# Seven block products in place of eight for the first layer of experts 1 to 7

## The chip, the cores and the metric

The kernel runs on one core of a Trainium2 chip. The metric is the device time of one execution in microseconds (us); a run gives one time, and a kernel's time is the median of its runs. The engines are PE (TensorE), DVE (VectorE), ACT (ScalarE), POOL (GpSimd) and SP (SyncE, which only issues transfers here). Each takes its instructions from a queue in the order in which the program wrote them; semaphores order the engines among each other.

## What is computed

Attention over 8 batches of 512 tokens with 256 features comes first, then a soft mixture of 8 experts with 128 slots each. The change is in the experts' part, which in the reference reads:

```python
slots = jnp.einsum('bnd,bnes->besd', xn, dispatch)
h = jnp.einsum('besd,edh->besh', slots, w1) + b1[None, :, None, :]
h = jax.nn.gelu(h, approximate=False)
eo = jnp.einsum('besh,ehd->besd', h, w2) + b2[None, :, None, :]
out = jnp.einsum('bmd,bnm->bnd', eo.reshape(b, e * s, DIM), combine)
```

For one expert, h is a product of 8 x 128 slot rows with 256 features and a w1 of 256 x 1024; eo multiplies it with a w2 of 1024 x 256.

## The kernel before

Matmuls take float32r. For accuracy each value is split in a rounded high part and the rest, and a product is made of three passes, high x high, high x low, low x high (`PASSES`). ACT rounds (a Copy to float32r), and DVE subtracts the rounded from the whole to get the rest: for weights `round_weights` (L1464) and `rest_of_weights` (L2077), for slots `round_slots` (L2084) and `rest_of_slots` (L2088), for hidden values L1499 and `rest_of_act` (L2120).

The kernel has three stages: attention and routing until some 381 us, the experts to some 738 us, and the combine. The slots of an expert lie in `slots_eo` with features on the partitions, as two halves (batches 0 to 3 and 4 to 7) of 512 columns and two feature blocks of 128. An expert is done in 16 steps i: half f = i // 8, hidden tile j = i % 8 of 128 rows. `hidden` makes the tile in one of four PSUM banks, 6 matmuls of 512 columns (two feature blocks, three passes). ACT applies Gelu to it into `act` (L1494) and rounds it into `act_r`, DVE forms the rest. Two steps later `expert_out` multiplies the tile, 128 slots at a time, with w2: one matmul of 512 columns that holds both parts of w2 (L1043) and one of 256 (L1046), into banks 4 to 7. The 512 columns there are two sums, high and low, which `keep_eo` adds when the half is done, with the bias b2 (eight DVE instructions of 256 elements; the result goes over the slots that are no longer needed). Only the first half of expert 0 has `narrow_out` (L1021), three matmuls of 256 columns.

The weights come into `stage`, w1 and w2 of 1 MB each, one raw copy at a time; the split parts have two buffers each, so those of expert e + 1 are made during expert e, at steps written out by hand (`ROUND_AT`, `REST_AT`). w2 is centred by its row means on DVE (`sum_rows`, `mean_of_rows`, `centre_rows`). SP loads the next pair when both splits are done. `eng.nop` in `alone` stands ahead of an instruction whose addresses come from a loop register.

POOL normalises dispatch weights (L617) and forms the rest of y (L624) in the routing, beside DVE's running minimum (L1953) and its comb shift with a PSUM input (L1962). It has no instruction in the expert stage except at its very start.

## Time and profile before

| | |
|---|---|
| median of 3 runs | 836.92 us (836.79 to 837.07) |
| profiled execution | 836.86 us, span 834.7 us |
| PE busy | 826.5 us (99%) |
| DVE busy | 643.2 us (77%) |
| ACT busy | 548.1 us (66%) |
| POOL busy | 86.3 us (10%) |
| PE in the chain that ended last | 95% |

The span is the time from the first to the last instruction of one profiled execution. Busy is the union of an engine's instructions. Matmuls are pipelined, so that one's recorded duration is longer than the step from its start to the next one's start; the step is what it costs. The same holds, by less, for DVE and ACT.

### The profile page before, as it was taken

The numbers are of one execution on the slowest core, as the hardware profiler recorded it, in microseconds if no ns is written. First come the engines' busy times: TensorE is split into PE (matmuls) and PEld (weight loads), VectorE is DVE, ScalarE is ACT, GpSimd is POOL, SyncE is SP. The second block draws the span as 40 slices with busy tenths as digits, with TensorE's granted clock in tenths as the row PEclk, the third lists the DMA queues.
The fourth block names the chain that finished last, engine by engine and source line by source line (L and its number), as shares of the span: only waits on it lengthen the run. The fifth ranks groups of instructions, "written<-read, shape, count | busy, mean of one in ns | idle before, by whom it ended". The sixth has DMA issues, their size and how long they took to land.

```text
span 834.7 us, 14932 instructions
## 1 busy us (share of the span) xinstructions
PE 826.5 (99%) x4866; PEld 717.7 (86%) x4866; DVE 643.2 (77%) x1293; ACT 548.1 (66%) x1078; POOL 86.3 (10%) x103
## 2 busy tenths in 40 slices
PE   8999999999999999999999999999999999999998
PEld 8989999888888888878888888888888888899997
DVE  8788888799999999898867666666766665477776
ACT  5666766657787887789555565555555554568775
POOL 0200000033223324450000000000000000000000
PEclk9999999999999999999999999999999999999999
DMA  7011131102323252125030303020110203066893
GB/s 235 33 51 52 51 101 31 47 26 90 109 95 126 89 201 98 68 89 202 1 102 0 101 1 101 0 89 11 38 62 0 101 0 101 1 213 211 284 285 117
DMA packets 52562, 75.38 MB, mean 90 GB/s; under 512 B 3104, under 2 KB 33696, under 8 KB 52384
## 3 DMA queue, kind: packets, MB, share of 16 engines
q1 hardware_dynamic: 52512, 74.76, 26.9%
q8 instruction: 26, 0.43, 0.2%
q14 instruction: 24, 0.20, 0.1%
HBM read 49.59 MB, written 25.17 MB: 90 GB/s over the span
## 4 chain that ended last, share of the span: by engine, by line
PE 95%; DVE 2%; ACT 1%; issue 1%; DMA 0%; ACTq 0%; DVEq 0%
PE bank L1013 21%; PE bank L1043 13%; PE bank L1085 11%; PE bank L882 10%; PE bank L907 10%; PE bank L1046 7%; PE bank L891 3%; PE bank L750 3%; PE bank L800 3%; PE bank L693 2%; PE bank L773 2%; PE bank L761 2%; PE bank L783 2%; PE bank L715 1%; PE bank L1021 1%; PE bank L726 1%
## 5 line engine op out<-in xcount | busy, mean ns | idle before, releaser
L1013 PE MATMUL bank<-snT,w_r 128*128 128x512 f32 x768 | 194.7, 393 | 0.0
L1494 ACT ACTIVATE act<-bank,b_sb 128x512 f32<-128x512 f32 x128 | 88.0, 687 | 139.1 <-PE bank L1013 138.7
L2120 DVE TENSOR_TENSOR act_r<-act,act_r 128x512 fp32r<-128x512 f32 x128 | 88.2, 690 | 110.8 <-ACT act_r L1499 110.6
L1043 PE MATMUL bank<-w_r,act_r 128*128 128x512 f32 x480 | 173.1, 396 | 0.0
L1013 PEld LDWEIGHTS bank<-snT,w_r 128*128 128x128 f32 x768 | 136.5, 188 | 28.8 <-issue 0.2
L1046 PE MATMUL bank<-w_r,act_r 128*128 128x256 f32 x480 | 134.5, 280 | 0.0
L1043 PEld LDWEIGHTS bank<-w_r,act_r 128*128 128x128 f32 x480 | 90.2, 188 | 21.1
L907 PE MATMUL bank<-disp_r,y_r 128*128 128x512 f32 x384 | 103.5, 406 | 0.4 <-DVE disp_r L1973 0.3
L882 PE MATMUL bank<-yT_r,snT 128*128 128x512 f32 x384 | 99.5, 395 | 0.0
L1046 PEld LDWEIGHTS bank<-w_r,act_r 128*128 128x128 f32 x480 | 90.6, 189 | 4.1
L1085 PE MATMUL bank<-eo_r,comb_r 128*128 128x258 f32 x768 | 92.3, 282 | 0.0
L1085 PEld LDWEIGHTS bank<-eo_r,comb_r 128*128 128x128 f32 x768 | 92.2, 189 | 0.1
L1499 ACT ACTIVATE act_r<-act 128x512 fp32r<-128x512 f32 x128 | 80.9, 632 | 12.0
L882 PEld LDWEIGHTS bank<-yT_r,snT 128*128 128x128 f32 x384 | 71.7, 188 | 16.0 <-issue 0.5
L907 PEld LDWEIGHTS bank<-disp_r,y_r 128*128 128x128 f32 x384 | 67.7, 189 | 12.9 <-DVE disp_r L1973 0.8
L1366 ACT ACTIVATE disp<-neg_lt,neg_max 128x512 f32<-128x512 f32 x56 | 40.5, 722 | 35.6 <-DVE neg_lt L1939 35.4
L617 POOL TENSOR_SCALAR disp<-disp,rz_disp 128x512 f32<-128x512 f32 x56 | 39.6, 707 | 124.0 <-DVE rz_disp L1968 124.0
L1973 DVE TENSOR_TENSOR disp_r<-bank,disp_r 128x512 fp32r<-128x512 f32 x64 | 43.5, 682 | 5.0 <-ACT disp_r L1378 4.4
L1393 ACT ACTIVATE comb<-comb,zero_col 128x512 f32<-128x512 f32 x64 | 45.4, 715 | 1.6 <-DVE comb L1962 1.4
L1378 ACT ACTIVATE disp_r<-bank 128x512 fp32r<-128x512 f32 x64 | 37.4, 585 | 10.8 <-PE bank L891 10.8
L1939 DVE TENSOR_SCALAR_CACHE_REDUCE neg_lt<-bank 128x512 f32<-128x512 f32 x56 | 38.3, 684 | 4.8 <-DVE comb L1962 2.5
L2077 DVE TENSOR_TENSOR w_r<-stage,w_r 128x1024 fp32r<-128x1024 f32 x32 | 38.9, 1218 | 0.0
(203 smaller groups left out, 1309.8 us busy)
## 6 DMA issues: line engine op xcount, KB each, us to landing
combine_scratch<-comb SPq DMA_DIRECT2D x64, 256.0 KB, 2.0
stage<-in_w SPq DMA_DIRECT2D x16, 1024.0 KB, 6.3
stage<-combine_scratch SPq DMA_DIRECT2D x4, 2048.0 KB, 9.1
snT<-combine_scratch SPq DMA_DIRECT2D x4, 2048.0 KB, 9.5
x_scratch<-stage SPq DMA_DIRECT2D x8, 512.0 KB, 3.1
x<-x_scratch SPq DMA_DIRECT2D x8, 512.0 KB, 4.0
x_d<-x_scratch SPq DMA_DIRECT2D x8, 512.0 KB, 9.4
slots_eo<-in_x SPq DMA_DIRECT2D x7, 512.0 KB, 4.5
```

Of the source, the lines that this page charges most:

```text
L882: last = pe.matmul(bank[m % 2][:, :], snT[:, i, k, m * S:(m + 1) * S], yT_r[:, j, k, :], start=(n == 0), stop=(n == len(steps) - 1))
L907: last = pe.matmul(bank[4 + k][:, :], y_r[:, i, t, k * P:(k + 1) * P], disp_r[h][:, j, t, :], start=(n == 0), stop=(n == len(fill_steps) - 1))
L1013: last = pe.matmul(hidden_bank(e, i)[:, :], w1_r[q][:, a, k, j * P:(j + 1) * P], sl_r[f][:, c, k, :], start=(n == 0), stop=(n == len(steps ...
L1043: pe.matmul(bank[BH + c][:, :].rearrange("p (w d) -> p w d", w=2), act_r[:, i % RING, 0, c * S:(c + 1) * S], w2_r[q][:, :, j, :], start=(j ...
L1046: pe.matmul(bank[BH + c][:, 0:D], act_r[:, i % RING, 1, c * S:(c + 1) * S], w2_r[q][:, 0, j, :], start=False, stop=(j == KH - 1), skip_gro ...
L1085: done = pe.matmul(bank[4 * u + t][:, 0:DZ], comb_r[:, m % RING, i, t * P:(t + 1) * P], eo_r[u][:, j, m, :], start=(m == 0 and n == 0), st ...
L1366: act_fn(dispatch(b, m), neg_logits(b, m), ACT.Exp, bias=least, scale=-1.0, accum_out=total).then_inc(disp_exp, 1)
L1393: act_fn(comb[:, m % RING, :], comb[:, m % RING, :], ACT.Exp, bias=zero_col[:], scale=-1.0)\
L1494: act_fn(act[:, i % 2, :], hidden_bank(e, i)[:, :], ACT.Gelu, bias=b1_sb[:, ds(e * KH + i % KH, 1)])\
L1499: act_fn(act_r[:, i % RING, 0, :], act[:, i % 2, :], ACT.Copy).then_inc(h_hi, 1)
L1973: v.tensor_tensor(disp_r[h][:, 1, :, cols], bank[2 + m % 2][:, :].rearrange("p (t s) -> p t s", t=NT), disp_r[h][:, 0, :, cols].bitcast(F3 ...
L2120: v.tensor_tensor(act_r[:, i % RING, 1, :], act[:, i % 2, :], act_r[:, i % RING, 0, :].bitcast(F32), ALU.subtract).then_inc(h_split, 1)
```

## The change

Expert 0 keeps its 16 steps, with all outputs narrow. For experts 1 to 7 the first layer is done in four groups of four tiles. A group is a 2 x 2 block product over a 2 x 2 block of w1 (two feature blocks, hidden tiles g and g + 4) and a 2 x 2 block of slots (two feature blocks, two halves), in Strassen's form as Winograd wrote it: seven products in place of eight, from four sums of w1 blocks and four of slot blocks. A product is three matmuls of 512 columns. Three pieces are common to several tiles: the chain bank collects P0, P2, P4 and P5, and ACT copies it out after P0, P2 and P4 (`keep_part`) into the tile's place in `act`; DVE adds the product in bank 3 or 1 to it (`add_tile`); Gelu then reads `act`, or for one tile of the four the bank.

The sums of blocks are made on POOL (`combine_w1`, in part in place in the raw w1; `combine_slots`), as is the high part of four slot operands (`cast_slots`), the centring of w2 and the rest of half of w2. All outputs are narrow, with the two halves of an expert in banks 4, 5 and 6, 7. w1's split operands have two buffers, one per parity of the group, and w2's have one. w1 and w2 load on semaphores of their own: w2 after its rest is done, w1 after the last group's `rest_of_w1`.

```diff
+        LEFT_AT = [0, 2, 4, 1, 5, 3, 6]
+        TILE_OF = [0, 2, 1, 3]
+        OUT_NEEDS = [1, 3, 3, 4]
...
+            with sp.Fori(2, E) as e:
+                sp.wait_ge(w_split[1], 2 * e)
+                load_w2(e)
+                sp.wait_ge(w_split[0], fills_through(e, 0, 0))
+                load_w1(e)
...
+            def combine_w1(e, g):
+                pool.wait_ge(w_loaded[0], 16 * (e + 1))
+                if not is_batch(e, 1) or g >= 2:
+                    pool.wait_ge(w_split[0], fills_through(e, g - 2, 2))
...
+                nc.gpsimd.tensor_tensor(s3, w1_block(0, 0, g), w1_block(0, 1, g), ALU.subtract).then_inc(w1_summed, 1)
...
+                nc.gpsimd.tensor_tensor(w1_block(0, 1, g), w1_block(0, 1, g), w1_block(1, 1, g), ALU.add)\
+                    .then_inc(w1_summed, 1)
...
+                nc.gpsimd.tensor_tensor(s2, w1_block(0, 1, g), w1_block(0, 0, g), ALU.subtract).then_inc(w1_summed, 1)
...
+                nc.gpsimd.tensor_tensor(s4, w1_block(1, 0, g), s2, ALU.subtract).then_inc(w1_summed, 1)
...
+            def cast_slots(e, n):
+                right_free(pool, e, n)
+                pool.wait_ge(sl_summed, 4 * (e - 1) + 4)
+                alone(pool)
+                nc.gpsimd.tensor_scalar(slot_operand(n)[:, 0], slot_source(e, n), 1.0, 1.0, ALU.mult, ALU.mult)\
+                    .then_inc(sl_cast, 1)
+
+            def expert(e, last=False):
+                combine_w1(e, 1)
+                for n in (4, 5):
+                    cast_slots(e, n)
+                pool.wait_ge(w_hi[1], 2 * e + 1)
+                alone(pool)
+                nc.gpsimd.tensor_tensor(w2_pairs(w2_r[:, 1], 0), w2_pairs(w2_raw, 0),
+                                        w2_pairs(w2_r[:, 0], 0).bitcast(F32), ALU.subtract).then_inc(w_split[1], 1)
+                combine_w1(e, 2)
+                if not last:
+                    combine_slots(e + 1)
+                combine_w1(e, 3)
+                if not last:
+                    combine_w1(e + 1, 0)
+                    for n in (2, 3):
+                        cast_slots(e + 1, n)
+                    centre_rows(e + 1)
...
+            def product(e, g, n):
+                if n == 0:
+                    pe.wait_ge(w_split[0], fills_through(e, g, 2))
+                if g == 0:
+                    pe.wait_ge(sl_split, right_through(e, [1, 1, 2, 3, 4, 6, 5][n]))
+                if n == 1:
+                    pe.wait_ge(h_act, tiles_through(e, g, -1))
+                elif n == 3:
+                    pe.wait_ge(h_act, tiles_through(e, g, 0))
+                elif n in (2, 4, 5):
+                    pe.wait_ge(part_kept, added_through(e, g, {2: 1, 4: 2, 5: 3}[n]))
+                elif n == 6:
+                    pe.wait_ge(tile_added, added_through(e, g, 2))
+                x = chain_bank(g)
+                target = [x, bank[3], x, bank[1], x, x, bank[1]][n]
+                for s, (a, c) in enumerate(PASSES):
+                    done = pe.matmul(target[:, :], w1_op[:, g % 2, a, LEFT_AT[n], :], slot_operand(n)[:, c, :],
+                                     start=(n in (0, 1, 3) and s == 0), stop=(s == 2), skip_group_check=True)
+                done.then_inc(h_in_psum, 1)
...
+            def expert_group(e, g, before):
+                product(e, g, 0)
+                product(e, g, 1)
+                before(0)
+                product(e, g, 2)
+                product(e, g, 3)
+                before(1)
+                product(e, g, 4)
+                before(2)
+                product(e, g, 5)
+                product(e, g, 6)
+                before(3)
...
+            def keep_part(e, g, i):
+                sc.wait_ge(h_in_psum, products_through(e, g, 2 * i + 1))
+                if i < 2:
+                    sc.wait_ge(h_split, tiles_through(e, g, -1 + i))
+                act_fn(act[:, [0, 3, 2][i], :], chain_bank(g)[:, :], ACT.Copy).then_inc(part_kept, 1)
...
+            def add_tile(e, g, i):
+                tile = [0, 2, 3][i]
+                dve.wait_ge(part_kept, added_through(e, g, [1, 3, 2][i]))
+                dve.wait_ge(h_in_psum, products_through(e, g, [2, 5, 7][i]))
+                v.tensor_tensor(act[:, tile, :], bank[3 if i == 0 else 1][:, :], act[:, tile, :], ALU.add)\
+                    .then_inc(tile_added, 1)
```

`before(a)` is the narrow output of tile a of the group before. The queue of DVE in one group:

```diff
+            def expert_group(e, g, first=False, last=False):
+                add_tile(e, g, 0)
+                if g:
+                    rest_of_tile(e, g - 1, 3)
+                elif not first:
+                    rest_of_tile(e - 1, GROUPS - 1, 3)
+                if g == 0:
+                    rest_of_operand(e, 4)
+                    split_last_operand(e)
+                if g == 1:
+                    keep_eo(e - 1, 1)
+                if g == GROUPS - 1 and not last:
+                    cast_first_two(e + 1)
+                    rest_of_first_two(e + 1)
+                rest_of_tile(e, g, 0)
+                if g == 0:
+                    rest_of_operand(e, 5)
+                if g < GROUPS - 1:
+                    rest_of_w1(e, g + 1, 0)
+                elif not last:
+                    rest_of_w1(e + 1, 0, 0)
+                add_tile(e, g, 1)
+                if g < GROUPS - 1:
+                    rest_of_w1(e, g + 1, 1)
+                elif not last:
+                    rest_of_w1(e + 1, 0, 1)
+                if g == 0 and not first:
+                    keep_eo(e - 1, 0)
+                if g == 1:
+                    rest_of_w2(e)
+                if g == 2 and not last:
+                    sum_rows(e + 1, 0)
+                    sum_rows(e + 1, 1)
+                if g == GROUPS - 1 and not last:
+                    rest_of_operand(e + 1, 2)
+                add_tile(e, g, 2)
+                rest_of_tile(e, g, 1)
+                if g == GROUPS - 1 and not last:
+                    rest_of_operand(e + 1, 3)
+                if g == 2 and not last:
+                    mean_of_rows(e + 1)
+                rest_of_tile(e, g, 2)
```

That of ACT:

```diff
+            def expert_group(e, g, first=False, last=False):
+                if g:
+                    gelu(e, g - 1, 3)
+                elif not first:
+                    gelu(e - 1, GROUPS - 1, 3)
+                keep_part(e, g, 0)
+                if g:
+                    round_tile(e, g - 1, 3)
+                elif not first:
+                    round_tile(e - 1, GROUPS - 1, 3)
+                gelu(e, g, 0)
+                keep_part(e, g, 1)
+                round_tile(e, g, 0)
+                if g < GROUPS - 1:
+                    round_w1(e, g + 1, 0)
+                    round_w1(e, g + 1, 1)
+                elif not last:
+                    round_w1(e + 1, 0, 0)
+                    round_w1(e + 1, 0, 1)
+                keep_part(e, g, 2)
+                if g < 2:
+                    round_w2(e, g)
+                gelu(e, g, 1)
+                round_tile(e, g, 1)
+                gelu(e, g, 2)
+                round_tile(e, g, 2)
```

## Rows read from the trace of the kernel before

**Rows 1.** The page: busy time by engine, and the chain that ended last.
```profile
PE 826.5 (99%) x4866; PEld 717.7 (86%) x4866; DVE 643.2 (77%) x1293; ACT 548.1 (66%) x1078; POOL 86.3 (10%) x103
PE 95%; DVE 2%; ACT 1%; issue 1%; DMA 0%; ACTq 0%; DVEq 0%
```

**Rows 2.** Windows: one steady expert; last columns are granted clock, DMA share, GB/s.
```profile
451.39:495.95 44.56, 44.56 (x226) 37.60 (x225) 29.21 (x46) 24.75 (x37) 0.00 (x0) 1.00 0.14 48
```

**Rows 3.** Timeline of PE: start, duration, engine, line, instruction, count.
```profile
440.24 1.55 PE L1013 MATMUL bank<-snT,w_r 128*128 128x512 f32 x6
441.63 0.39 PE L1043 MATMUL bank<-w_r,act_r 128*128 128x512 f32 x1
...
443.03 0.86 PE L1013 MATMUL bank<-snT,w_r 128*128 128x512 f32 x3
```

**Rows 4.** Timeline of PE in expert 0, with narrow outputs.
```profile
391.24 1.59 PE L1021 MATMUL bank<-w_r,act_r 128*128 128x256 f32 x12
392.67 1.55 PE L1013 MATMUL bank<-snT,w_r 128*128 128x512 f32 x6
```

**Rows 5.** Timelines of PE, ACT and DVE behind one hidden tile.
```profile
484.80 1.55 PE L1013 MATMUL bank<-snT,w_r 128*128 128x512 f32 x6
486.19 0.39 PE L1043 MATMUL bank<-w_r,act_r 128*128 128x512 f32 x1
...
486.56 0.69 ACT L1494 ACTIVATE act<-bank,b_sb 128x512 f32<-128x512 f32 x1 [1.35 <-PE bank L1013]
487.37 0.63 ACT L1499 ACTIVATE act_r<-act 128x512 fp32r<-128x512 f32 x1
487.90 1.04 ACT L1464 ACTIVATE w_r<-stage 128x1024 fp32r<-128x1024 f32 x1
...
488.03 0.69 DVE L2120 TENSOR_TENSOR act_r<-act,act_r 128x512 fp32r<-128x512 f32 x1 [0.89 <-ACT act_r L1499]
488.64 1.22 DVE L2183 TENSOR_TENSOR stage<-stage,w_mean 128x1024 f32<-128x1024 f32 x1
```

**Rows 6.** Groups by line and form, DVE: busy us, mean ns of one, idle before.
```profile
L2077 DVE TENSOR_TENSOR w_r<-stage,w_r 128x1024 fp32r<-128x1024 f32 x32 | 38.9, 1218 | 0.0
...
L1962 DVE TENSOR_TENSOR comb<-neg_lt,bank 128x512 f32<-128x512 f32 x56 | 37.3, 673 | 0.2
...
L2084 DVE CAST snT<-slots_eo 128x1024 fp32r x12 | 8.3, 688 | 0.0
```

**Rows 7.** POOL's lines and sources: duration in ns, least, median and most.
```profile
L624 POOL TENSOR_TENSOR y_r<-y,y_r x16: 1274/1503/1777, 169.4 to 369.1; 128x512 fp32r<-128x512 f32 x16
...
L617 POOL TENSOR_SCALAR disp<-disp,rz_disp x56: 684/693/1122, 184.4 to 372.3; 128x512 f32<-128x512 f32 x56
...
L609 POOL TENSOR_SCALAR slots_eo<-slots_eo,se_scale x8: 472/492/508, 30.1 to 33.4; 128x256 f32<-128x256 f32 x8
...
L604 POOL TENSOR_SCALAR stage<-stage,b_mean x1: 926/926/926, 27.2 to 27.2; 128x256 f32<-128x256 f32 x1
```

**Rows 8.** Timelines of POOL and DVE in the routing stage, where both work.
```profile
195.97 1.30 POOL L624 TENSOR_TENSOR y_r<-y,y_r 128x512 fp32r<-128x512 f32 x1
...
196.24 1.57 DVE L1953 TENSOR_TENSOR run_min<-run_min,neg_lt 128x512 f32<-128x512 f32 x1
197.74 0.68 DVE L1973 TENSOR_TENSOR disp_r<-bank,disp_r 128x512 fp32r<-128x512 f32 x1
...
223.23 0.69 POOL L617 TENSOR_SCALAR disp<-disp,rz_disp 128x512 f32<-128x512 f32 x1 [2.01 <-DVE rz_disp L1968]
223.89 1.72 POOL L624 TENSOR_TENSOR y_r<-y,y_r 128x512 fp32r<-128x512 f32 x1
...
223.56 0.90 DVE L1953 TENSOR_TENSOR run_min<-run_min,neg_lt 128x512 f32<-128x512 f32 x1
```

**Rows 9.** DMA issues: KB each, median us from issue to landing.
```profile
stage<-in_w SPq DMA_DIRECT2D x16, 1024.0 KB, 6.3
```

## What the change does to the time: the prediction

> **What bounds the kernel now.** I read the page first: TensorE is busy for 826.5 of 834.7 us and holds 95% of the chain that ended last [rows 1]. Next the windows: a steady expert takes 44.56 us, with PE busy all of it at the full granted clock (1.00, the 2.4 GHz level), DVE 29.21, ACT 24.75 and POOL nothing [rows 2]. Then the timeline of PE, where the start of the next group gives the true cost of one, since the matmuls' own durations overlap. Six matmuls of 512 columns (`hidden`) take 441.63 - 440.24 = 1.39 us, 0.232 each, and the eight of `expert_out` 443.03 - 441.63 = 1.40 [rows 3]. So this stage costs what its matmuls cost, and a change in it is worth their number, as long as nobody makes PE wait. The queues of DVE, ACT and POOL show how near that is.
>
> The sum is made against the profiled execution: 836.86 us, 834.7 of it span. The median of the runs is 836.92, so the two can be used alike. A difference under 0.2% (1.7 us) can't be told from none.
>
> **PE's own work.** A group of four hidden tiles costs 44.56 / 4 = 11.14 [rows 2]. Now it has seven products of three 512-column matmuls, 7 x 0.695 = 4.87, and four narrow outputs. The trace has those: twelve matmuls of 256 columns take 392.67 - 391.24 = 1.43 [rows 4], 0.03 more than the wide form. 4.87 + 4 x 1.43 = 10.59 us a group; 0.55 less, times 28 groups (7 experts x 4) = -15.4. The second half of expert 0 turns narrow too: 8 x 0.03 = +0.2. **PE alone: -15.2**, with 588 products' matmuls where there were 672.
>
> **Engine work, one expert.** Prices first. An instruction of 512 elements on DVE lasts 0.69, and the next starts 0.61 after it (488.03 to 488.64); ACT's Gelu starts 0.37 after PE's slot ends (486.19 to 486.56), its copy 0.81 after that and lasts 0.63, and DVE follows within 0.03 [rows 5]. An add with a PSUM input is 0.67, 1024 elements 1.22, a 1024 cast 0.69 [rows 6]. DVE gets 12 `add_tile`, halves `keep_eo` (four PSUM adds in place of 16), and gives two centrings and half a w2 rest to POOL: 16 rests and 12 adds (28 x 0.61), w1 rests 4 x (0.61 + 0.48), slot operands 5 x 0.61 + 1.14 + casts 0.97, w2 1.14, `keep_eo` 4 x 0.6, sums 2.4: 32.5 of 42.4 us. ACT gets 12 `keep_part` of at most 0.63: 16 x (0.81 + 0.53) + 12 x 0.55 + w1 4.2 + w2 2.0 is near 34 (the next instruction starts 0.53 after a copy, 487.37 to 487.90). Neither is a bound by its share.
>
> POOL had no work here and gets 27 instructions per expert: 16 `tensor_tensor` of 128 elements, 4 of 512, 3 of 1024, 4 casts of 512. The trace has 512 at 1.274 and a `tensor_scalar` at 0.684, and 0.472 to 0.492 for 256 [rows 7]. The latter two give 0.26 to 0.30 fixed, say 0.28; the rest of 1.28 over 512 elements is 1.95 ns each, so I estimate 0.53 for 128 and 2.28 for 1024. Bounds for the 128: 0.28 (the fixed part alone) and 0.93 (the slow `tensor_scalar` of 256) [rows 7]. I take 0.53, from the row of the same operation. Total: 8.5 + 5.1 + 6.8 + 2.8 = 23.2.
>
> **The port.** In [rows 8], a DVE `tensor_tensor` with two SBUF inputs (L1953) begins at 196.24 while POOL's runs from 195.97 to 197.27, and takes 1.57 in place of 0.68: it did its work after POOL. At 223.56 to 224.46 it waits for POOL again, and POOL's next, from 223.89, takes 1.72 in place of 1.29: held back 0.43. PSUM adds go on beside POOL unharmed (197.74: 0.68). So POOL and DVE's two-SBUF-input instructions exclude each other; of the latter an expert has 16 + 8 + 6 + 1, some 19.5 us. With POOL's 23.2 that is 42.7 for one resource, already PE's 42.4, before any order is asked of it.
>
> The Trainium skill says the same (SBUF — State Buffer, section "SBUF: two separate sides"): the pair of ports is an exclusive lock held for a whole instruction, against DVE instructions with two SBUF inputs. The trace agrees; taking each hold as the whole 0.61 instead of a mean of 0.52 would add 0.8 us an expert and put the sum 5 us higher.
>
> **The order.** On a group's clock PE starts P0 at 0, P1 0.70, first output 1.39, P2 2.82, P3 3.52, P4 5.64, P5 7.77, P6 8.46, next group 10.6. Follow the one w1 buffer. In group 2, `keep_part` follows P4 (6.34 + 0.37 + 0.63 = 7.34), `add_tile` 1 ends at 8.05, and `rest_of_w1` for group 3, the last reader of w1, ends near 8.55. Only then does SP load the next w1: 6.3 us [rows 9], so it lands at 14.85, 4.25 into group 3. ACT has `round_w1` for the next expert just there, ahead of the third `keep_part`, on which P5 waits. Behind the load POOL does in order four sums, two casts, two centrings, four sums and cast 4: 8 x 0.57 + 3 x 0.69 + 2 x 2.32 = 11.3 with 0.04 for each hand-over, as from ACT to DVE. That ends 15.55 into group 3, 4.95 into group 0 of the next expert. DVE stands at `rest_of_operand(e, 4)` from about 3.0 in that group, and behind it in its queue are the split of operand 6, the rest of tile 0, operand 5, `rest_of_w1` and `add_tile` 1: 4.1 us, to 9.1 or so. P6 waits for that add and is due at 8.46. **Without any port conflict the group is 0.7 late.**
>
> With it: between 4.25 in group 3 and 3.0 in group 0 DVE issues nine two-input instructions (the rest of the first two operands, four tile rests, two of w1, operands 2 and 3), and each holds POOL back 0.43 to 0.61. 9 x 0.52 = 4.7. The same POOL work has the next w1's sums late for ACT, and a centring of 2.28 sits in front of `rest_of_w1`, on which the next P0 waits; these stalls are part of the same delay, not more. **5.4 us for each of six transitions between experts 1 to 7: +32.4.** From both sides: 0 if POOL is fast and free, 0.7 without conflicts, 5.4, and with 0.93 for the small sums 8 x 0.4 = 3.2 more.
>
> Group 1: POOL goes on with the w2 rest, sums, `combine_slots` (4 x 1.28) and sums, and never pauses. DVE has 1.8 adds, 2.4 rests, 1.1 w1, 1.2 `keep_eo`, 1.1 w2 = 7.7 there, seven of its instructions with two SBUF inputs. Each meets a POOL instruction part way; the wait lies between 0 and the 0.89 of [rows 8]. At 0.6, DVE needs 11.9 against 10.6: **+1.3 in each of 7 experts, 9.1.** Group 2 is nearly free of POOL and works the queue down: 0.
>
> First group of expert 1: no outputs stand between P4, P5 and P6, so P5 waits 1.05 for `keep_part`, and the first output waits for POOL's w2 rest, another 0.6: **+1.7**. Operands 2 and 3, cast only after the last `hidden`, come 0.3 ahead of P2. At the end PE has 5.7 us of outputs before `combine(0, 0)`; both halves of `eo_r` and the first combine tiles fit in behind them, the load of combine rows being issued two groups earlier: 0. The transfers that moved (w2 ahead of w1, on its own semaphore) come within group 2, ahead of the sums of its rows: 0; were w2 late, 2.3 us of sums would queue in front of `add_tile` 2.
>
> Sum: -15.2 + 32.4 + 9.1 + 1.7 = +28.0, so **864.9 us**.
>
> **Rivals.** (a) The gain stays, 24 in 100. POOL's idle 15 us per expert absorb the conflicts, or DVE, once it waits for cast 4, leaves POOL the port, so that the delay shrinks to the 0.7 of the bare order: -15.2 + 1.7 + 6 x 0.7 = -9.3, 827.6; with sums at their lower bound 823. It decides from a delay below 13.5 / 6 = 2.25 us a transition. For it: the port shows in one pair of lines of the trace only. Against: eleven microseconds of POOL in one chain, and 9.1 against 8.46 with no conflict at all.
> (b) Half the conflicts, 12 in 100 slower and 4 in 100 no change: group 1 keeps up, transitions cost 3.2: -15.2 + 1.7 + 19.2 = +5.7, 842.6.
> (c) POOL's small sums cost 0.93, 10 in 100: 6 x 3.2 = 19 more, 884.
> (d) The forecast, 50 in 100: 852 to 876.
>
> Slower (b, c, d) 0.72, same 0.04, faster (a) 0.24. The range takes in (a)'s 827 and (c)'s 884; in the forecast's own case it is 852 to 876.
>
> **What would show it.** A product line with 588 matmuls at 0.232 and outputs at 0.119 a matmul: PE's work. Expert period 47 to 50 us against 44.56; PE idle ahead of products, released by DVE operands and `tile_added` in group 0; DVE idle in front of the rest of operand 4, released by a POOL cast; DVE's tile rests with a mean above 0.69, PSUM adds at 0.67; POOL's `tensor_tensor` of 512 above 1.28. Wrong if POOL's chain from w1's landing to cast 4 is under 12 us, or if the two-input instructions keep 0.69.

## The result, and the profile after

The changed kernel takes 865.63 us (median of 4 runs, 863.20 to 867.27) against 836.94 for the kernel before beside it (836.79 to 837.07). The ratio is 1.0342, with a 95% interval of 1.0330 to 1.0354. The profiled execution took 865.51 us, 863.7 of it span. The page of the changed kernel, first the busy time of the engines, then the rows of the costliest groups that the forecast had named (busy us, mean ns of one, idle time before them and who ended it):

```profile
PE 829.5 (96%) x5262; PEld 736.7 (85%) x5262; DVE 734.4 (85%) x1336; ACT 602.9 (70%) x1204; POOL 282.7 (33%) x292
...
L1221 PE MATMUL bank<-snT,w_op 128*128 128x512 f32 x336 | 94.8, 420 | 23.0 <-ACT act L1695 21.4
...
L2430 DVE TENSOR_TENSOR act_r<-act,act_r 128x512 fp32r<-128x512 f32 x112 | 88.9, 805 | 14.1 <-ACT act_r L1715 13.8
...
L1221 PE MATMUL bank<-w_first,w_op 128*128 128x512 f32 x252 | 70.6, 402 | 1.8 <-DVE w_first L2367 0.8
...
L2423 DVE TENSOR_TENSOR act<-bank,act 128x512 f32<-128x512 f32 x84 | 57.6, 686 | 37.6 <-ACT act L1695 33.1
```

Against [rows 1], POOL has gone from 86.3 to 282.7 us and DVE from 643.2 to 734.4. The 336 + 252 = 588 matmuls of the products are there. DVE's tile rests (L2430, two SBUF inputs) have a mean of 805 ns where [rows 5] had 690, and its adds with a PSUM input (L2423) keep 686. PE now waits 21.4 us for ACT's L1695, which is `keep_part`.

The windows of one steady expert, cut at the start of each group's first product; the second row is a whole group, the next four are the pieces of group 0. Columns are length, busy time of PE, weight load, DVE, ACT and POOL, then granted clock, DMA share, GB/s:

```profile
506.05:554.96 48.91, 45.06 (x278) 40.10 (x277) 42.28 (x53) 32.68 (x55) 28.32 (x27) 0.97 0.13 43
...
508.05:519.36 11.31, 11.13 (x72) 9.61 (x70) 10.39 (x14) 7.48 (x13) 7.63 (x8) 1.00 0.21 85
519.36:525.40 6.04, 3.08 (x20) 2.61 (x18) 5.36 (x5) 2.00 (x4) 5.61 (x7) 1.00 0.00 0
525.40:528.13 2.73, 2.73 (x6) 2.16 (x7) 2.55 (x5) 2.24 (x5) 0.37 (x1) 0.51 0.00 0
528.13:529.88 1.75, 1.75 (x14) 1.75 (x13) 1.75 (x4) 1.01 (x3) 0.00 (x0) 0.79 0.00 0
529.88:534.82 4.94, 4.94 (x36) 4.55 (x34) 3.77 (x7) 3.79 (x6) 2.36 (x1) 1.00 0.00 0
534.82:545.40 10.58, 10.58 (x71) 9.68 (x70) 9.62 (x11) 8.47 (x15) 9.53 (x10) 1.00 0.00 0
545.40:556.96 11.56, 10.86 (x72) 9.75 (x70) 8.85 (x12) 7.70 (x14) 2.81 (x4) 1.00 0.37 101
```

An expert takes 48.91 us against 44.56 [rows 2]. PE's own group is 10.58, seen whole in group 1 (534.82), as forecast. Group 3 (508.05) is 0.7 over it. Group 0 is the sum of the four pieces, 15.46, 4.9 over. Group 2 (545.40) is 1.0 over. In group 0, PE idles 2.96 before its third product; the six matmuls behind that take 2.73 in place of 1.39 [rows 3], and the outputs 1.75 in place of 1.43 [rows 4]. In those two pieces the granted clock is 0.51 and 0.79, that is, at first the 1.2 GHz level and then a mix of it with 2.4 GHz. So 1.34 + 0.32 = 1.7 us of the 4.9 are a slower PE, and about 3.2 are the wait and the start behind it.

The timeline of the same stretch, all engines; each row is start, duration, engine, line, instruction, count, and in brackets the idle time before it and who ended it:

```profile
511.30 0.46 POOL L748 TENSOR_TENSOR w_sum<-stage 128x128 f32<-128x128 f32 x1 [11.55 <-DMA stage<-in_w]
...
514.88 2.07 POOL L775 TENSOR_SCALAR snT<-sl_sum 128x512 fp32r<-128x512 f32 x2
...
516.92 4.07 POOL L767 TENSOR_TENSOR stage<-stage,w_mean 128x1024 f32<-128x1024 f32 x2
516.99 2.23 DVE L2384 TENSOR_TENSOR w_op<-w_sum,w_op 128x384 fp32r<-128x384 f32 x1
...
519.15 2.38 DVE L2367 TENSOR_TENSOR snT<-sl_sum,snT 128x512 fp32r<-128x512 f32 x1
...
521.45 0.68 DVE L2423 TENSOR_TENSOR act<-bank,act 128x512 f32<-128x512 f32 x1
...
522.34 0.72 ACT L1707 ACTIVATE act<-act,b_sb 128x512 f32<-128x512 f32 x1 [2.29 <-DVE act L2423]
...
523.78 0.94 DVE L2430 TENSOR_TENSOR act_r<-act,act_r 128x512 fp32r<-128x512 f32 x1
524.14 1.63 POOL L775 TENSOR_SCALAR w_first<-sl_sum 128x512 fp32r<-128x512 f32 x2
524.75 0.60 ACT L1695 ACTIVATE act<-bank 128x512 f32<-128x512 f32 x1 [1.69 <-DVE act_r L2430]
...
525.40 2.93 PE L1221 MATMUL bank<-snT,w_op 128*128 128x512 f32 x6 [2.96 <-ACT act L1695]
...
526.68 0.69 DVE L2367 TENSOR_TENSOR w_first<-sl_sum,w_first 128x512 fp32r<-128x512 f32 x1
```

Read it from the bottom. PE's third product waits for ACT's `keep_part` 0 (524.75), which frees the bank. ACT waits there 1.69 for DVE's rest of the previous group's third tile (523.78): `keep_part(e, g, 0)` waits for `h_split` up to that tile, although the tile that it overwrites had been done with earlier. DVE is late because `add_tile` 2 of the previous group starts only at 521.45. Ahead of it DVE has two instructions with two SBUF inputs, the rest of w1's sums (516.99) and the rest of operand 2 (519.15), and they take 2.23 and 2.38 us. They begin beside POOL's two centrings of 1024 elements (516.92 to 520.99). POOL itself began at 511.30, when w1 landed, after 11.55 us of idling. The casts of operands 4 and 5 (524.14, two instructions), of which the forecast had cast 4 in this place, are both done by 525.77, and DVE's rest of operand 4 (526.68) is not held up by them. Group 2 has its 1.0 from the same wait of `keep_part` 0: PE idles 0.70 ahead of the third product there.

```profile
549.08 1.65 PE L1221 MATMUL bank<-snT,w_op 128*128 128x512 f32 x6 [0.70 <-ACT act L1695]
```

### The profile page after: what moved, and what is told of

Its sections match the earlier page's. It is cut to its first block and busy times, and to the rows that moved or that the text cites. A ratio compares the mean times of both kernels' runs of the same rounds, so it can differ in the third digit from the quotient of the medians.

```text
span 863.7 us, 16838 instructions
## 1 busy us (share of the span) xinstructions
PE 829.5 (96%) x5262; PEld 736.7 (85%) x5262; DVE 734.4 (85%) x1336; ACT 602.9 (70%) x1204; POOL 282.7 (33%) x292
## 5 line engine op out<-in xcount | busy, mean ns | idle before, releaser
L1179 PEld LDWEIGHTS bank<-w_r,act_r 128*128 128x128 f32 x1536 | 204.5, 194 | 12.6 <-DVE act_r L2415 1.8
L1179 PE MATMUL bank<-w_r,act_r 128*128 128x256 f32 x1536 | 207.0, 286 | 1.4 <-DVE act_r L2415 1.4
L1221 PE MATMUL bank<-snT,w_op 128*128 128x512 f32 x336 | 94.8, 420 | 23.0 <-ACT act L1695 21.4
L2430 DVE TENSOR_TENSOR act_r<-act,act_r 128x512 fp32r<-128x512 f32 x112 | 88.9, 805 | 14.1 <-ACT act_r L1715 13.8
L1707 ACT ACTIVATE act<-act,b_sb 128x512 f32<-128x512 f32 x84 | 60.7, 723 | 52.6 <-DVE act L2423 51.8
L1221 PEld LDWEIGHTS bank<-snT,w_op 128*128 128x128 f32 x336 | 62.8, 199 | 36.7 <-ACT act L1695 23.7
L1276 PEld LDWEIGHTS bank<-eo_r,comb_r 128*128 128x128 f32 x768 | 92.1, 189 | 0.4 <-DVE comb_r L2455 0.4
L2423 DVE TENSOR_TENSOR act<-bank,act 128x512 f32<-128x512 f32 x84 | 57.6, 686 | 37.6 <-ACT act L1695 33.1
L1695 ACT ACTIVATE act<-bank 128x512 f32<-128x512 f32 x84 | 49.8, 593 | 46.6 <-PE bank L1221 25.5
L1221 PE MATMUL bank<-w_first,w_op 128*128 128x512 f32 x252 | 70.6, 402 | 1.8 <-DVE w_first L2367 0.8
L1221 PEld LDWEIGHTS bank<-w_first,w_op 128*128 128x128 f32 x252 | 43.5, 192 | 11.8 <-DVE act L2423 3.6
L748 POOL TENSOR_TENSOR w_sum<-stage 128x128 f32<-128x128 f32 x28 | 24.9, 888 | 70.6 <-DMA stage<-in_w 70.6
```

The source lines that it names most:

```text
L1179: done = pe.matmul(bank[BH + 2 * f + c // 2][:, (c % 2) * D:(c % 2 + 1) * D], act_r[:, tile, a, c * S:(c + 1) * S], w2_r[:, w, j, :], star ...
L1221: done = pe.matmul(target[:, :], w1_op[:, g % 2, a, LEFT_AT[n], :], slot_operand(n)[:, c, :], start=(n in (0, 1, 3) and s == 0), stop=(s = ...
L1276: done = pe.matmul(bank[4 * u + t][:, 0:DZ], comb_r[:, m % RING, i, t * P:(t + 1) * P], eo_r[u][:, j, m, :], start=(m == 0 and n == 0), st ...
L1695: act_fn(act[:, [0, 3, 2][i], :], chain_bank(g)[:, :], ACT.Copy).then_inc(part_kept, 1)
L1707: act_fn(act[:, tile, :], chain_bank(g)[:, :] if i == 2 else act[:, tile, :], ACT.Gelu, bias=b1_sb[:, ds(e * KH + j, 1)]).then_inc(h_act, 1)
L2423: v.tensor_tensor(act[:, tile, :], bank[3 if i == 0 else 1][:, :], act[:, tile, :], ALU.add)\
```

## The experiments

Twelve kernels were run, each beside the kernel before on the same chip (836.80 to 836.88 us there). All numbers are medians.

**1. POOL nearly out of it.** All POOL instructions of an expert work on 8 columns from expert 2 on, and the two centrings on 2 columns a row for every expert; the same instructions and waits remain.

```diff
-nc.gpsimd.tensor_tensor(t3, slots_raw(e, 1, 1), slots_raw(e, 0, 1), ALU.subtract)
+nc.gpsimd.tensor_tensor(t3[:, 0:width(e)], slots_raw(e, 1, 1)[:, 0:width(e)], ...)
...
-nc.gpsimd.tensor_scalar(slot_operand(n)[:, 0], slot_source(e, n), 1.0, 1.0, ALU.mult, ALU.mult)
+nc.gpsimd.tensor_scalar(slot_operand(n)[:, 0, 0:width(e)], slot_source(e, n)[:, 0:width(e)], ...)
```

> From expert 2 on, every POOL instruction of the expert stage works on 8 columns only (sums, slot casts, centring, half of the w2 rest), so the values of these experts are not the reference's; order, waits and the work of the other engines stay. Theory A (POOL and DVE's instructions with two SBUF inputs exclude each other, and POOL's long ones stop DVE): the stalls of experts 2 to 7 go, PE runs these groups in 10.6 us, and the time falls to about 836.9 - 15.2 + 5 (first groups of expert 1) = 827. Theory B (the order of the queues alone costs, above all a copy of the chain bank that waits for rests): a delay of over 2.3 us stays at each change of expert, 840 or more.

Measured: 825.35 us, ratio 0.9867 (0.9850 to 0.9883). The windows of a steady expert of this kernel (columns as above):

```profile
444.00:486.35 42.35, 42.35 (x277) 38.74 (x277) 33.30 (x53) 32.54 (x54) 9.38 (x27) 1.00 0.15 51
```

PE is busy all of it, at 10.59 a group. The seven products are worth what the forecast gave them, and all that stands against them, 865.63 - 825.35 = 40.3 us, hangs on the length of POOL's instructions. This kernel does not tell the port from the chain: shorter instructions ease both.

**2 and 3. The centrings: the port, or the chain.** The second kernel cuts the two centrings to 2 columns a row. The third puts two constant fills in the place of each, which read nothing and last together about as long. Neither centres w2 as the reference needs it, so neither gives its values.

```diff
-nc.gpsimd.tensor_tensor(rows, rows, means.unsqueeze(3).to_broadcast([P, 2, 2, D]), ALU.subtract)
+nc.gpsimd.memset(rows, 0.01).then_inc(w2_centred, 2)
+...
+nc.gpsimd.memset(rows, 0.02).then_inc(w2_centred, 2)
```

> Only the two centrings of w2 on POOL are cut to 2 columns of each row (w2 stays almost uncentred). They take 4.1 us in group 3 just as DVE has two rests to make. Both theories: the idle time of 3.0 us before P2 in group 0, and the slow matmuls behind it (1.7 us in the profiled expert), go in most of the six changes of expert: 6 x 4 = 24 us less, about 842. If the centring is not what stops DVE: no change, 865.

> The two centrings of w2 on POOL are replaced by two fills each with a constant of the same rows (w2 is then constant), which read nothing from SBUF and should last about as long (0.9 us each by the fixed part and one element a cycle; the trace will tell). Theory A: only a POOL instruction that reads SBUF keeps DVE's two-input instructions out, so DVE's rests beside the fills keep 0.69 and the time is that of the run without centring, about 842. Theory B (POOL's chain from w1's landing to the casts is too long): POOL is as long busy as before, 865.

Measured: 836.20 us without the centrings' work, ratio 0.9992 (0.9982 to 1.0002), 29.4 less than the changed kernel. With fills 854.48, ratio 1.0209 (1.0192 to 1.0226), between the two expectations. The timeline of the kernel with fills says why:

```profile
560.35 0.95 POOL L767 MEMSET stage<- 128x1024 f32 x1
...
560.45 0.54 DVE L2386 TENSOR_TENSOR w_op<-w_sum,w_op 128x384 fp32r<-128x384 f32 x1
560.92 0.68 DVE L2369 TENSOR_TENSOR snT<-sl_sum,snT 128x512 fp32r<-128x512 f32 x1
...
571.39 2.39 POOL L786 TENSOR_TENSOR w_r<-stage,w_r 128x1024 fp32r<-128x1024 f32 x1 [3.35 <-ACT w_r L1732]
...
572.03 2.16 DVE L2386 TENSOR_TENSOR w_op<-w_sum,w_op 128x384 fp32r<-128x384 f32 x1
...
579.31 1.95 PE L1223 MATMUL bank<-snT,w_op 128*128 128x512 f32 x6 [1.87 <-ACT act L1697]
```

The same two instructions of DVE that took 2.23 and 2.38 beside the centrings take 0.54 and 0.68 beside fills, though POOL's chain is as long (four fills of 0.95 for two centrings of 2.03): what stops them is a POOL instruction that reads SBUF. The Trainium skill states this condition (SBUF — State Buffer, section "SBUF: two separate sides": two SBUF inputs lock DVE out only against a GpSimd instruction that reads SBUF); the trace agrees, 0.68 against 2.38. But the order then goes wrong one group later. POOL's w2 rest (571.39) now meets the rest of w1's sums (572.03, 2.16), and PE waits 1.87 in group 1. The port is shown; as a size, the 11.2 us between the fills and the centrings (865.63 - 854.48) are not its whole cost, since the fills only move part of the stall.

**4. Narrow outputs alone.** In the kernel before, all outputs take the narrow form in four banks, without the products.

```diff
-                if first and f == 0:
-                    narrow_out(q, i, j)
-                    return
+                if j == 0 and not (first and f == 0):
+                    pe.wait_ge(eo_ready, e * HALVES * BH + (f - 1) * BH)
+                narrow_out(q, i, j)
+                return
```

> The kernel before, with one part of the change: all outputs of experts as three matmuls of 256 columns, the halves of an expert in banks 4, 5 and 6, 7, and the sums kept in four instructions. By the forecast 120 steps cost 0.03 us more each: +3.6, 840.5. Rival: the weight loads (three for two) bound the narrow form when DVE and ACT are busier, some 0.1 us a step: 849; or the DVE's shorter keeping gives it back: 837.

Measured: 840.37 us, ratio 1.0042 (1.0025 to 1.0059), 3.5 more. The 0.03 us per output from [rows 3] and [rows 4] hold (3.5 / 120).

**5. The clock.** Twelve matmuls that feed nothing stand ahead of the third product in group 0 (experts 2 to 7), where PE waits anyhow.

```diff
                 before(0)
+                if g == 0 and not is_batch(e, 1):
+                    for _ in range(12):
+                        pe.matmul(bank[2][:, :], w1_op[:, 0, 0, LEFT_AT[1], :], slot_operand(1)[:, 0, :], ...)
                 product(e, g, 2)
```

> Twelve more matmuls of 512 columns (2.8 us of PE, results never read) ahead of P2 in group 0 of experts 2 to 7, where PE is idle for about 3.0 us. Theory C (the granted clock falls to 1.2 GHz after that idle time, and P2, P3 and the next outputs pay up to 1.7 us): PE stays busy, the clock stays at 1.00, and the kernel gets faster by 0.5 to 1.7 us at each of six places: 855 to 862, with less spread. Without theory C: same time, 865, since the fill only covers idle time.

Measured: 857.86 us, ratio 1.0249 (1.0232 to 1.0267), 7.8 less than the changed kernel, with a mean granted clock of 1.00 in place of 0.986. Group 0 takes 13.75 where it took 15.46: the 1.7 us that the windows above gave to the clock. Over the six groups 0 the sum falls from 92.1 to 83.6 us. Another 1.5 us come from a place that the edit does not touch, the second group of expert 1, where both kernels have the same instructions and the same waits ahead of it, and only the granted clock differs (first the changed kernel, then this one); groups 2 and 3 take back some 2 us:

```profile
436.40:448.80 12.40, 12.40 (x70) 10.96 (x70) 10.73 (x13) 8.35 (x15) 10.81 (x12) 0.86 0.01 3
...
436.67:447.58 10.91, 10.91 (x69) 9.75 (x70) 10.14 (x12) 8.31 (x15) 9.61 (x10) 1.00 0.01 2
```

**6, 7 and 8. Moving the work, loosening the wait.** The sixth kernel has the centrings behind casts 4 and 5, in group 0. The seventh lets the first `keep_part` of a group wait for the tile alone that it overwrites (expert 1's first group keeps the old wait). The eighth does both.

```diff
                 for n in (4, 5):
                     cast_slots(e, n)
+                if not first:
+                    centre_rows(e)
...
-                    centre_rows(e + 1)
```

```diff
-                    sc.wait_ge(h_split, tiles_through(e, g, -1 + i))
+                    sc.wait_ge(h_split, tiles_through(e, g, -1 + i if is_batch(e, 1) and g == 0 else 3 * i - 3))
```

> The same work: POOL centres w2 of expert e after the casts of operands 4 and 5 in group 0, where it idles for 6.7 us in the profile, instead of at the end of the expert before. Theory A: the rests in group 3 meet no long POOL instruction, P2 waits no longer; in group 0 one or two DVE rests are stopped by up to 2 us, of which PE sees part: 3 us less per change of expert, 847. Theory B: about 865, as POOL has the same work.

> The first copy of the chain bank waits only for the rest of the tile whose place it takes, not for two more. In the profile it starts 1.7 us after the Gelu that is ahead of it, waiting for the third tile rest. Theory B (this wait is the one that ends last): 1.7 us and part of the clock's loss in each of six changes, and 0.7 in group 2: 15 us less, 851. If the stopped DVE alone decides, through the add in front of that Gelu: under 3 us less.

> The centring later, and the first copy with the looser wait. Both theories together: the idle times before P2 go, 0.7 to 2 us of others stay: 840 to 845.

Measured: 863.24 (ratio 1.0307, 1.0289 to 1.0324), 857.77 (1.0247, 1.0229 to 1.0264) and 855.11 us (1.0221, 1.0204 to 1.0238). All three missed what was expected. The seventh is no faster than the fifth (857.77 against 857.86), which keeps the old wait and only holds the clock up, so these runs do not show that the looser wait gives more than the clock does. The timeline of the sixth kernel:

```profile
521.29 4.63 POOL L767 TENSOR_TENSOR stage<-stage,w_mean 128x1024 f32<-128x1024 f32 x2
...
524.09 2.38 DVE L2368 TENSOR_TENSOR w_first<-sl_sum,w_first 128x512 fp32r<-128x512 f32 x1
...
526.60 0.95 PE L1222 MATMUL bank<-w_first,w_op 128*128 128x512 f32 x3 [0.97 <-DVE w_first L2368]
```

The centrings stop another rest of DVE, that of operand 4, again for 2.38 us, and another product waits. The table of group lengths further down shows the same for all three: most of what group 0 gains, group 1 loses.

**9 and 10. Three long instructions taken off POOL.** ACT's rounding of w2 takes the mean off itself (Identity with a bias), and DVE takes the mean off in the same instruction as the rest; POOL's centrings and its half of the w2 rest are gone. ACT and DVE make the first half of w2's split one group earlier, in group 3 of the expert before (for expert 1, whose predecessor has no such group, in its own group 0). The ninth kernel has the loosened wait too, the tenth hasn't.

```diff
+                for j in w2_rows(c):
+                    done = v.scalar_tensor_tensor(out=w2_r[:, 1, j, :], in0=w2_raw[:, j, :],
+                                                  scalar=w2_mean[:, j:j + 1], in1=w2_r[:, 0, j, :].bitcast(F32),
+                                                  op0=ALU.add, op1=ALU.subtract)
```

> The same results by other work: w2 is centred inside its split. ACT rounds four rows at a time as Identity with the negative row mean as bias (256 elements each, 8 instructions for 2 of 1024), DVE forms the rest as (w2 - mean) - high (8 instructions of 256 for one of 1024), the first half of it one group earlier; POOL loses its three instructions of 1024 elements (6.5 us per expert), and the first copy of the chain bank has the looser wait. Theory A and B together: with the long POOL instructions gone no place is left where PE waits over 0.5 us but expert 1's first groups (5 us): 836.9 - 15.2 + 5 + 6 x 0.7 = 831, faster than both kernels. If the small sums and casts on POOL alone still stop DVE's rests, or DVE with 34 of 42.4 us is now late by itself: 840 or more.

> The same without the looser wait of the first copy. Theory B (that wait costs by itself): 5 us or more above the run with it. Theory A (it only passes on how late DVE is): within 2 us of it.

Measured: 848.29 (ratio 1.0142, 1.0125 to 1.0159) and 856.56 us (1.0242, 1.0225 to 1.0259). The ninth was expected at 831, or at 840 and more if what is left on POOL, or DVE by itself, still stalls PE: the second came. The wait by itself is worth 8.3 us once POOL is lighter, as the tenth was expected to show, most of it in group 1 (10.74 against 12.07); here the mean granted clock is alike in both (0.996 and 0.998). What is left in the ninth kernel is a wait of 1.30 us before the fifth product of group 0 for `keep_part`, whose add stands behind four w2 rests on DVE:

```profile
521.08 2.49 DVE L2392 SCALAR_TENSOR_TENSOR w_r<-stage,w_mean,w_r 128x256 fp32r<-128x256 f32 x4
523.50 0.68 DVE L2426 TENSOR_TENSOR act<-bank,act 128x512 f32<-128x512 f32 x1
...
525.62 0.96 PE L1218 MATMUL bank<-w_first,w_op 128*128 128x512 f32 x3 [1.30 <-ACT act L1692]
```

**11 and 12. Starting w1 earlier, and those rests later.** The eleventh kernel adds to the ninth a w1 load that waits for the last instructions that read the loaded w1, and no longer for the rest of its sums (it is issued 3.8 to 4.0 us ahead of group 3 where the ninth has 1.7 to 1.9), and puts ACT's second rounding of w1 in group 3 behind the third `keep_part`. The twelfth is the eleventh with the first half of the w2 rest moved from group 3 into group 0, ahead of `keep_eo`.

```diff
-                sp.wait_ge(w_split[0], fills_through(e, 0, 0))
+                sp.wait_ge(w_split[0], fills_through(e, 0, 0) - 1)
+                sp.wait_ge(w1_summed, (e - 1) * 4 * GROUPS)
```

```diff
                 if g == 0 and not first:
+                    rest_of_w2(e, 0)
                     keep_eo(e - 1, 0)
```

> The kernel with w2 centred in its split and the looser wait, and two waits moved: SP loads the next w1 as soon as the last direct reader of it (step 0 of the rest for group 3, and all sums) is done, 2.4 us earlier in the profile, and in group 3 ACT copies the chain bank a third time before it rounds the sums of the next w1, for which it waited 1.6 us. The theory that POOL's chain behind the landing of w1 sets the end in group 3 and 0: up to 2 us less for each of six changes of expert, 838 to 842. If DVE's queue alone sets it (the split of w2 in front of the first add of group 0): at most 0.7 us each, 844 or more.

> As the one before, and the first half of w2's rest (2.5 us of DVE beside POOL's sums) moves from the end of group 3, ahead of the first add of group 0, to behind the second add of group 0, where no product of that group waits behind it. The theory that what is queued on DVE ahead of an add decides: P4 of group 0 no longer waits, 2 us less for each of six, 828 to 834 and faster than both kernels. If the total of DVE and the port is the limit: no gain, as the same work then delays group 1.

Measured: 846.00 (ratio 1.0107, 1.0092 to 1.0123) and 860.36 us (1.0283, 1.0269 to 1.0297). The eleventh gains 2.3 us on the ninth: not the 838 to 842 expected if w1's landing set the end, but the 844 or more of DVE's queue. Two things were changed at once, so that the 2.3 can't be given to either. The twelfth is 14.4 us slower than the eleventh, where it was hoped to win; what came is its rival, that the same work then delays group 1. The timeline of the twelfth kernel, the four rests of 256 elements once with POOL beside them and once, in group 1, without:

```profile
530.15 1.34 POOL L735 TENSOR_TENSOR sl_sum<-slots_eo 128x512 f32 x1 [0.24 <-POOL sl_sum L731]
530.25 5.05 DVE L2394 SCALAR_TENSOR_TENSOR w_r<-stage,w_mean,w_r 128x256 fp32r<-128x256 f32 x4
531.64 1.30 POOL L739 TENSOR_TENSOR sl_sum<-slots_eo,sl_sum 128x512 f32<-128x512 f32 x1
533.17 1.26 POOL L742 TENSOR_TENSOR sl_sum<-slots_eo,sl_sum 128x512 f32<-128x512 f32 x1 [0.23 <-POOL sl_sum L739]
...
536.55 2.92 PE L1177 MATMUL bank<-w_r,act_r 128*128 128x256 f32 x12 [3.30 <-DVE slots_eo L2447]
...
545.55 1.67 DVE L2394 SCALAR_TENSOR_TENSOR w_r<-stage,w_mean,w_r 128x256 fp32r<-128x256 f32 x4 [0.35 <-ACT w_r L1729]
```

Beside three POOL instructions of 1.3 us four short ones of DVE take 5.05 us in place of 1.67: about one of them gets in after each. `keep_eo` stands behind them and PE's outputs wait 3.30.

Group 0 alone was cured in this kernel (10.63). The lengths of the four groups from one w1 load to the next, worked out as differences of PE's group starts in each timeline, for one expert of each kernel, show where each kernel has its stalls (it varies from expert to expert: group 0 of the changed kernel takes 13.98 to 16.56):

```
kernel                 group 3  group 0  group 1  group 2   sum
changed kernel          11.31    15.46    10.58    11.56   48.91
 2 centrings cut        11.10    10.57    10.60    11.80   44.07
 3 fills                11.23    11.64    14.24    10.58   47.69
 5 matmuls in the gap   11.72    13.75    10.59    11.84   47.90
 6 centrings later      11.72    13.12    13.10    10.58   48.52
 7 loosened wait        11.06    13.40    12.54    10.59   47.59
 8 both                 11.07    13.12    12.33    10.59   47.11
 9 w2 off POOL, loose   11.41    12.73    10.74    10.59   45.47
10 w2 off POOL          11.45    12.89    12.07    10.58   46.99
11 w1 earlier           10.96    12.55    10.74    10.58   44.83
12 w2 rests later       11.23    10.63    15.67    10.58   48.11
```

The best version that computes everything, the eleventh, still loses to the kernel before: 44.83 us an expert against 44.56 [rows 2] (44.71 is its mean from expert 2 to expert 7), 846.00 against 836.82. But the steady experts are not where most of the 9.2 us lie. Expert 1 takes 50.8 us in it, from its first product to that of expert 2, where it takes 43.1 in kernel 1. Its second group takes 18.73 us (17.4 to 18.7 in kernels 9 to 12, 12.40 in the changed kernel), because two rests of DVE beside POOL take 3.46, the first half of w2's rest for expert 1 follows only then, and the outputs wait for it:

```profile
435.40 3.46 DVE L2435 TENSOR_TENSOR act_r<-act,act_r 128x512 fp32r<-128x512 f32 x2
...
438.79 2.46 DVE L2394 SCALAR_TENSOR_TENSOR w_r<-stage,w_mean,w_r 128x256 fp32r<-128x256 f32 x4
...
441.34 2.90 PE L1177 MATMUL bank<-w_r,act_r 128*128 128x256 f32 x12 [4.20 <-issue]
```

The outputs start 0.09 after that rest ends (438.79 + 2.46 = 441.25), and the granted clock is 0.50 from there to 446.60. With kernel 1's start, 7.6 us less, the eleventh kernel would be near 838; that is an estimate, and was not run.

## Why the prediction was right, and where its steps were not

Predicted were 864.9 us, slower; measured 865.63. The direction is as forecast. The mechanism (POOL's SBUF-reading instructions against DVE's with two SBUF inputs) is shown by kernels 1 and 3 together; the chain behind the one w1 buffer, along which the forecast laid it, is read from the timeline. That the total agrees within a microsecond is partly luck: terms offset each other, and the six transitions, the largest term, hold some 8.5 us of a slower clock that the forecast did not have (kernel 5). Point by point:

- **PE alone, -15.2.** Right. A group without waits is 10.58 against 10.59. With POOL cut (kernel 1) 825.35 - 836.88 = -11.5 is left; the first group of expert 1, which that kernel leaves whole, has 3.3 of waits in it (below), and the second 0.3 (10.89), so PE's part is -15.1.
- **Six transitions, +32.4.** Group starts on PE's timeline give, over 10.59, 0.48, 0.72, 0.57, 0.58, 0.54 and 0.58 in the six groups 3, and 4.84, 4.87, 5.97, 4.87, 4.61 and 3.40 in the groups 0 behind them: 3.5 + 28.6 = 32.1. The size came out, the path in group 0 was not the one forecast. The forecast had DVE standing at the rest of operand 4 for POOL's cast, and P6 waiting for `add_tile` 1. Neither happened; the sixth and seventh products had no wait. What happened was two rests of DVE stopped by the centrings for 2.2 and 2.4 us, a late `add_tile` 2, and `keep_part` 0 waiting for a tile rest that it need not wait for. The forecast had named the centring as one of the stalls, but took it as part of the same delay. Nor did it name the over-strict wait. w1 lands 3.25 into group 3 (511.30 - 508.05), not 4.25, as its load takes 5.1 us on the page where [rows 9] had 6.3; POOL's chain from there to the end of cast 4 takes 13.9 us (511.30 to 525.19; 11.3 + 4.7 = 16.0 forecast), above the 12 that would have spoken against it.
- **Price of a conflict, 0.52.** Too even. Most rests lost about 0.25 (0.94 for 0.69), and the two beside the centrings 1.7 each. The nine-by-0.52 sum gave 4.7 a transition, but 1.7 of the 5.6 measured in the one shown is the clock's.
- **The clock.** Not forecast. PE's wait in group 0 was followed by a granted clock of 0.51, which cost 1.7 us in the transition shown. Kernel 5, whose clock stays at 1.00, is 7.8 us faster; 1.5 of the difference arise in the second group of expert 1.
- **Group 1, +1.3 in seven experts, 9.1.** The place was wrong, and the size too large. Group 1 of the steady experts has no wait. DVE's backlog shows one group later, 1.0 in group 2 of five experts, which is 4.9 us, through the over-strict wait of `keep_part` 0; with that wait loosened (kernel 7) group 2 is 10.59. Another 1.8 are in group 1 of expert 1, but 1.5 of them are the clock (12.40 against 10.91 in kernel 5) and only 0.3 a stall. Together 6.7 us.
- **First group of expert 1, +1.7.** Undersized: it took 3.3. The timeline of PE there:

```profile
432.62 0.95 PE L1221 MATMUL bank<-w_first,w_op 128*128 128x512 f32 x3 [0.78 <-DVE w_first L2367]
433.89 0.93 PE L1221 MATMUL bank<-w_first,w_op 128*128 128x512 f32 x3 [0.33 <-DVE act L2423]
436.40 1.01 PE L1221 MATMUL bank<-snT,w_op 128*128 128x512 f32 x2 [1.58 <-DVE w_op L2384]
```

  P5 (432.62), which was forecast to wait 1.05 for `keep_part`, waits for DVE's rest of operand 5, P6 for its add, and P0 of the next group for the rest of w1's sums. This last wait is the port once more, and was not in the term: that rest takes 2.68 us (0.56 in expert 0, at 413.60) beside POOL's rest of w2:

```profile
433.57 2.37 POOL L784 TENSOR_TENSOR w_r<-stage,w_r 128x1024 fp32r<-128x1024 f32 x1 [3.90 <-ACT w_r L1730]
433.66 2.68 DVE L2384 TENSOR_TENSOR w_op<-w_sum,w_op 128x384 fp32r<-128x384 f32 x1
```

- **Expert 0, nothing but 0.2.** Wrong by 1.6. In its second half the first outputs start at 412.53 where they were due at 410.93, waiting for a tile rest of DVE (L2415). DVE is late by the same pair: two of its two-input instructions (404.70, 5.76 us) beside POOL's first two centrings (404.22, 5.16). With the centrings cut (kernel 1) that wait is gone.
- **PSUM adds.** The row that the forecast read for them (197.74 in [rows 8]) starts after POOL's instruction had ended (197.27), so it did not show that they go on beside POOL. The changed kernel does: its 84 adds of L2423 have a mean of 686 ns.
- **POOL's prices.** 0.46 for 128 elements undisturbed, where 0.53 was estimated, and 2.03 for 1024, where 2.28 was. Rival (c), with 0.93 for the small sums, shows only where DVE holds them back.

Terms together: -15.2 + 32.1 + 6.7 + 3.3 + 1.6 = +28.5, and 865.63 - 836.94 = 28.7. The forecast's sum was +28.0, since group 1's term was 2.4 too large, the transitions' 0.3 too large, and the last two 3.2 too small.

Rival (a), that the gain stays, was right on PE's side (825.35 with POOL cut). POOL's idle time did not absorb the conflicts, as it lies in the wrong place: 11.55 us of it from group 2 to the landing of w1 in group 3, ahead of the whole chain, and none from there to the casts in group 0. Kernels 6 and 8 moved POOL's centrings, and kernel 12 a rest of DVE, and the stall moved with them. That the one w1 buffer is what decides is argued from this and not shown: kernel 11, which adds an earlier load to kernel 9, gained 2.3 us together with another edit. What stays open is whether a second w1 buffer, which would let the sums of the next expert start in group 2, wins; that was not tried.

## What to carry to other kernels

When a change gives TensorE fewer matmuls and an idle engine more preparation, add that engine's SBUF-reading time to the time of VectorE's instructions with two SBUF inputs, as one resource, before counting the gain; here the forecast's estimate of it was 42.7 us in a period of 42.4. Then look at when the idle engine may start, not how long it idles: with one buffer holding its start back, moving its instructions about only moved the stall here. The longest instructions beside VectorE's set the largest stalls: leaving out the two centrings was worth 29.4 us, and giving them and POOL's half of the w2 rest to ACT and DVE was worth 17.3, together with the looser wait. Splitting them was not tried. Last, look at the first round of a pipeline by itself: the best version has a steady round 0.15 us above the kernel before, and loses most of its 9.2 us before the steady state begins.

## What the hardware showed that had not been expected

- PE had six waits of 2.96 to 3.02 us in group 0, in a stage in which it was busy otherwise. Behind five of them the granted clock fell, to between 0.50 and 0.73 over the next 2.5 to 2.8 us, and behind one it did not. The windows behind the second and the last:

```profile
525.40:528.13 2.73, 2.73 (x6) 2.16 (x7) 2.55 (x5) 2.24 (x5) 0.37 (x1) 0.51 0.00 0
...
721.37:724.10 2.73, 2.73 (x17) 2.46 (x18) 2.63 (x5) 2.43 (x5) 0.31 (x1) 1.00 0.00 0
```

  Six matmuls of 512 in the first, seventeen matmuls in the second, in the same time. Of two waits of 1.87 and 1.86 us ahead of the same product one was followed by 0.84 and then 0.50 (kernel 3), the other by 1.00 (kernel 6). The waits of 0.78, 0.33 and 1.58 us in the first group of expert 1 were followed by 0.55 over the next 3.8 us in the changed kernel, and by 1.00 in kernel 5 after the same instructions and waits. So the length of the wait does not tell by itself; what else decides was not tried.
- Beside POOL instructions that follow one another, a DVE instruction with two SBUF inputs ended some 0.3 us after each of them (kernel 12), one for each. So a row of short ones loses the more: four of 256 elements took 5.05 us in place of 1.67.
- A POOL fill of 1024 elements takes 0.95 us, and leaves DVE's instructions at their 0.68.
- The changed kernel spreads by 4 us between runs (863.20 to 867.27), where the kernel before spreads by 0.3. The spread goes with the mean granted clock, 0.990 to 0.983.
